# A four-layer recurrent block on one core: the down projection becomes a woven stage, and the balancing's column product is taken by rows

## What is computed

```
xn = layernorm(x)
s  = attention_L(xn)              # four different attentions
g  = silu(feed_forward_L(xn))     # four different feed-forwards
x  = x + s * g
```

```
w_eff = w * (su @ sv)
d = silu(x @ gate_eff.T) * (x @ up_eff.T)
y = d @ down_eff.T
```

## Time and profile before

| | |
|---|---|
| median of 3 runs | 1273.21 us (1271.34 to 1274.51) |
| profiled execution | 1270.83 us, span 1268.8 us |
| granted TensorE clock, mean of the span | 0.908 |
| PE busy | 1050.2 us, 83% |
| DVE busy | 834.3 us, 66% |
| ACT busy | 565.0 us, 45% |
| POOL busy | 328.4 us, 26% |

### The profile page before, as it was taken

How to read it: one execution, slowest core, us unless ns; L and a number is a source line. 1 busy time by engine, 2 the same in 40 slices (tenths; PEclk the granted TensorE clock), 3 DMA queues, 4 the chain that set the end, 5 groups by cost and what they waited for, 6 DMA issues and landing times.

```text
span 1268.8 us, 19873 instructions
## 1 busy us (share of the span) xinstructions
PE 1050.2 (83%) x7480; PEld 444.8 (35%) x7480; DVE 834.3 (66%) x1475; ACT 565.0 (45%) x797; POOL 328.4 (26%) x516
## 2 busy tenths in 40 slices
PE   2889999897898997865535639899899988999998
PEld 2434444343333444531211302223233234434344
DVE  6322222001786884798997999888978787876874
ACT  2533333100565664502123335858645767354671
POOL 2145444001776311000002136360000042011230
PEclk9989999998698998786657758999999999999999
DMA  8421220001321011020000032140012111220200
GB/s 306 143 73 55 72 75 25 1 1 49 89 64 35 26 37 60 14 63 22 16 0 1 27 102 74 48 148 28 20 35 69 51 44 39 64 76 26 69 17 34
DMA packets 54899, 69.72 MB, mean 55 GB/s; under 512 B 9526, under 2 KB 43444, under 8 KB 54800
## 3 DMA queue, kind: packets, MB, share of 16 engines
q1 hardware_dynamic: 50828, 58.57, 14.7%
q0 software_dynamic: 3984, 9.98, 2.8%
HBM read 49.45 MB, written 18.82 MB: 54 GB/s over the span
## 4 chain that ended last, share of the span: by engine, by line
DVE 30%; PE 30%; issue 4%; ACT 4%; POOL 3%; DMA 3%; SPq 1%; ACTq 0%; DVEq 0%; POOLq 0%
DVE w_mx L1320 14%; PE w_banks L667 8%; PE w_po L1250 7%; PE w_banks L1230 4%; PE w_banks L1202 3%; DVE w_region L1933 2%; ACT w_pr L1270 2%; PE w_banks L1190 2%; PE w_banks L1584 2%; DVE w_region L1893 1%; DVE w_region L1930 1%; DVE w_region L1928 1%; DVE w_region L1926 1%; DMA w_ks<-stack_scratch 1%; DVE w_region L1924 1%
## 5 line engine op out<-in xcount | busy, mean ns | idle before, releaser
L1320 DVE TENSOR_REDUCE w_mx<-w_banks 128x2 f32<-128x1024 f32 (+3 forms) x352 | 368.6, 1086 | 94.0 <-PE w_banks L1202 92.6
L1270 ACT ACTIVATE w_pr<-w_banks 128x1024 f32<-128x1024 f32 (+1 forms) x312 | 304.2, 1014 | 214.3 <-PE w_banks L1230 201.9
L1308 POOL TENSOR_SCALAR_AFFINE_SELECT w_pr<-w_pr 128x512 f32<-128x512 f32 (+1 forms) x184 | 107.8, 591 | 396.1 <-ACT w_pr L1270 396.1
L1230 PE MATMUL w_banks<-w_qs,w_ks 49*128 49x512 f16 (+7 forms) x832 | 125.4, 346 | 42.9 <-DVE w_mx L1320 30.3
L1202 PE MATMUL w_banks<-w_ks,w_qs 48*128 48x512 f16 (+7 forms) x832 | 139.4, 351 | 25.1 <-DVE w_mx L1320 11.3
L1250 PE MATMUL w_po<-w_pr,w_vz 128*17 128x512 f32 (+7 forms) x1152 | 142.8, 533 | 17.1 <-DVE w_vz L909 6.7
L78 PE MATMUL f_pp<-xt,sl_region 128*128 128x512 f16 x672 | 149.2, 383 | 2.4 <-POOL sl_region L504 2.4
L480 DVE TENSOR_TENSOR sl_region<-sl_region,f_pp 128x512 f32<-128x512 f32 x28 | 19.3, 688 | 120.3 <-ACT sl_region L495 120.3
L78 PEld LDWEIGHTS f_pp<-xt,sl_region 128*128 128x128 f16 x672 | 65.2, 99 | 83.8 <-issue 5.6
L1230 PEld LDWEIGHTS w_banks<-w_qs,w_ks 49*128 49x128 f16 (+1 forms) x832 | 36.0, 97 | 147.1 <-issue 58.3
L1190 PE MATMUL w_banks<-mask_half,ident_half 64*128 64x128 bf16 (+1 forms) x768 | 64.7, 248 | 17.9 <-DMA w_ks<-stack_scratch 8.6
(11 more groups left out here) (221 smaller groups left out, 1478.9 us busy)
## 6 DMA issues: line engine op xcount, KB each, us to landing
stack_scratch<-sl_region SPq DMA_DIRECT2D x102, 128.0 KB
w_qs<-stack_scratch SPq DMA_DIRECT2D x96, 96.0 KB, 2.3
sl_region<-in_L_gu SPq DMA_DIRECT2D x14, 512.0 KB
w_stage<-in_L_w POOLq DMA_DIRECT2D x36, 128.0 KB, 2.4
sl_region<-in_L_down SPq DMA_DIRECT2D x14, 256.0 KB
stack_scratch<-p_qk SPq DMA_DIRECT2D x24, 128.0 KB
w_ks<-stack_scratch SPq DMA_DIRECT2D x32, 96.0 KB, 2.5
bw_stage<-in_L_w SPq DMA_DIRECT2D x4, 640.0 KB, 10.1
```

The source lines that it names most:

```text
L1230: mm = pe.matmul(g.banks.pair_at(f)[:, half, at:at + T - q0], g.ks[base:base + self.rows + 1, k_slot, k_place, j * P:(j + 1) * P], g.qs[ba ...
L1270: act.activation(g.probs.at(self.pr_fill[s])[:, :, 0:width], g.banks.pair_at(self.s_fill[s])[:, :, 0:width], ACT.Exp, scale=self.a.scale). ...
L1308: pool.affine_select(out=diagonal, in_=diagonal, compare_op=ALU.is_ge, fill=0.0, base=0, pattern=pattern, channel_multiplier=-1).then_inc( ...
L1320: dve.tensor_reduce(out, g.banks.pair_at(self.m_fill[m])[:, :, 0:heads * keys].rearrange("q h (p k) -> q h p k", k=keys), AX.X, ALU.max).t ...
```

## The change

1. `swiglu_low_rank` no longer has the phase d0. It calls `finish(dt, wd)`, which runs a new block, `down_and_maxima`.
2. In that block the down projection is a stage `Down` of 89 ticks, 11 for each of the 8 tiles (four matmuls each, two in the last) and one for the last silu. It is merged, by a table of its own, with the first 4 ticks of q, 18 of m and 3 of t of the first attention: three groups' maxima. The block has parts for PE, ACT, DVE and SP.
3. `clear_semaphores` still follows `first_layer`, and `weave` begins behind it. The weave's strands leave out the ticks already done (`rest_of`). Queries, keys, maxima and the PSUM banks of the weave are allocated before the first layer; otherwise the body of `weave` is the same, with its indentation changed.
4. Balancing's column product writes its tile row by row, with the inverses broadcast over the rows.
5. The table `TURNS` is new. The old one begins with ten w ticks, the new one with 2, then l, then 27. By count of ticks, balancing's first step stands in the old table where the projection p11 (layer 1, second batch) begins, and its last step 11 ticks of s ahead of the outward product o10 (layer 1, first batch), with that layer's scores and values all done. In the new one 41 steps stand ahead of p11, and o10 starts 6 steps before balancing's end, with 12 e and 16 v ticks of layer 1 still to come.

```diff
-        sl = view(g.sl_region, 0, (NT, D), F32)
-        with Phase(nc, "d0", "made silued") as (block, made, silued), \
-                nc.psum_tensor("d0_pf", [P, 4, BANK], F32) as pf:
...
-                for t in range(NT):
-                    wait_pos(pe, silued, t - 3)
-                    product(pe, pf[:, t % 4, :], lambda part, j: dt[:, part, j, t * P:(t + 1) * P],
-                            lambda part, j: wd[:, part, j, :], range(n_i)).then_inc(made, 1)
...
+        finish(dt, wd)
...
+class Down(Stage):
...
+        self.parts = -(-self.chunks * len(PRODUCTS) // 4)
+        s = g.signals
+        self.made, self.out = s.take("d_made", NT), s.take("d_out", NT)
+        self.ticks = range(NT * self.parts + 1)
...
+        mm = partial(pe, self.g.banks.at(self.fills[i]), lambda part, c: self.gated[:, part, c, i * P:(i + 1) * P],
+                     lambda part, c: self.w[:, part, c, :], range(self.chunks), PRODUCTS, 4 * k, 4 * k + 4)
+        if k == self.parts - 1:
+            mm.then_inc(self.made.sem, 1)
+
+    def act(self, act, t):
+        i, k = divmod(t, self.parts)
+        if k == 0 and i > 0:
+            act.wait_ge(self.made.sem, self.made.at + i)
+            act.activation(self.sl[:, i - 1, :], self.g.banks.at(self.fills[i - 1]), ACT.Silu).then_inc(self.out.sem, 1)
...
         elif step == 5:
-            op = dve.tensor_tensor(bycol, bycol, inverse.rearrange("p (t j) -> p t j", j=n).unsqueeze(3)
+            whole = both.rearrange("p t (i j) -> p t i j", j=n)
+            op = dve.tensor_tensor(whole, whole, inverse.rearrange("p (t j) -> p t j", j=n).unsqueeze(2)
                                    .to_broadcast([P, NT, n, n]), ALU.mult)
...
+FIRST_TURNS = "q4 d6 " + "m1 d5 " * 6 + "t1 " + "m1 d5 " * 6 + "t1 d2 " + "m1 d3 " * 6 + "t1 d3"
+
 TURNS = """
-    w10 m5 q m2 q2 l m t m q m3 e m e t m e m e m2 v e m v e q e v t w2 q e o m2 v m e m v m e2 o m w v e2 w v m w e
...
+    w2 l w27 e q e2 q e2 v e2 v2 m e m2 e2 v m2 o m v o e2 v m e v e v m o m t m v e o v2 e m v o m q e2 o m2 t e m
...
+def rest_of(stage, emitted):
+    return stage, [t for t in stage.ticks if (stage, t) not in emitted]
...
         load_constants(nc, g, ins)
-        first_layer(nc, g, ins, x_tiles, by_chunk)
+        first_layer(nc, g, ins, x_tiles, by_chunk, lambda gated, w: down_and_maxima(nc, top, g, stacks[0], gated, w))
         clear_semaphores(nc)
         weave(nc, top, g, ins, out, stacks, by_chunk, sign_region, sign_qkv, sign_o)
+
+
+def down_and_maxima(nc, top, g, stack_dram, gated, w):
+
+    banks = top.enter_context(nc.psum_tensor("w_banks", [P, 7, BANK], F32))
+    g.po = top.enter_context(nc.psum_tensor("w_po", [P, BANK], F32))
...
+    down = Down(g, gated, w, view(g.sl_region, 0, (NT, D), F32))
+    g.first = first = Attend(g, g.heads[0], 0, g.vz0[:, 0:NI, :, :], g.att[:, 0:NI, :], stack_dram, None, None)
+    order = []
+    merge({"d": [all_of(down)], "q": [some_of(first.stacks, 0, SLOTS + 1)], "m": [some_of(first.maxima, 0, SLOTS * first.n_m)],
+           "t": [some_of(first.turns, 0, SLOTS)]}, FIRST_TURNS, order, g.emitted, g.banks)
+    with nc.Block() as block:
+        @block.tensor
...
+        @block.scalar
...
+        @block.vector
...
+        @block.sync
...
```

More of the change, by code:

```diff
@@ L1941 @@
[L1941 to L1950, removed]
@@ new lines, in split_rows, with done @@
+    def split_rows(name, dst, chunks=KC):
+        return [(by_chunk(name, chunks)[:, c, :], dst[:, 0, c, :], dst[:, 1, c, :]) for c in range(chunks)]
+    def done(stage):
+        return stage.normed, stage.groups
+    a00 = g.first
+    a01 = Attend(g, h[0], 1, vz(0, 1), att(1), stacks[0], None, a00)
+    split1 = Split(g, split_rows("L0_wo", wo) + split_rows("L1_w", w1)
+                   + split_rows("L1_wo", wo1, 2) + split_rows("L1_w24", w24) + [(ins["L1_wb"], wb[:, 0], wb[:, 1])])
+    o00 = Outward(g, h[0], 0, lambda part, c: wo[:, part, c, :], o_rows[:, 0, :], att(0), sl[:, 0], done(a00), None,
+                  [split1.done(), small.done()])
@@ new lines, in weave @@
+    n20 = Normalise(g, 0, (o10.added, NI), att(0))
+    p20 = Project(g, h[2], 0, lambda part, c, cols: sign_qkv[:, c, cols], g.binary.cols, g.binary.rows[:, 0:h[2].n_v],
+                  vz(2, 0), n20, stacks[2], [])
+    a20 = Attend(g, h[2], 0, vz(2, 0), att(0), stacks[2], p20, a11)
+    split2 = Split(g, split_rows("L2_w_ra", w_ra) + [(ins["L2_w_b"], w_b[:, 0, :], w_b[:, 1, :])])
+    o11 = Outward(g, h[1], 1, lambda part, c: wo1[:, part, c, :], o_rows[:, 1, :], att(1), sl[:, 1], done(a11),
+                  s1.ready(), [])
@@ new lines, in weave @@
+    n21 = Normalise(g, 1, (o11.added, NI), att(1))
+    p21 = Project(g, h[2], 1, lambda part, c, cols: sign_qkv[:, c, cols], g.binary.cols, g.binary.rows[:, 0:h[2].n_v],
+                  vz(2, 1), n21, stacks[2], [])
+    a21 = Attend(g, h[2], 1, vz(2, 1), att(1), stacks[2], p21, a20)
+    r20 = Routed(g, 0, w_ra, w_b, 1, sl[:, 0], n20, [split2.done(), small.done()], [(o10.gated, NI)])
+    split3 = Split(g, split_rows("L3_w", w3) + split_rows("L3_wo", wo),
+                   [(p11.made, len(p11.chunks)), (p11.v_made, p11.v_units), s1.ready(), (o01.made, NI)])
@@ new lines, in weave @@
+    p30 = Project(g, h[3], 0, lambda part, c, cols: w3[:, part, c, cols], col3, v_row3[:, :], vz(3, 0), n30, stacks[3],
+                  [split3.done(), rows3.done(), small.done()] + rope_free, rope=True)
+    a30 = Attend(g, h[3], 0, vz(3, 0), att(0), stacks[3], p30, a21)
+    r21 = Routed(g, 1, w_ra, w_b, 1, sl[:, 0], n21, [], [(o20.gated, NI)])
+    r21.begins_after = [(o20, o20.ticks[-1])]
+    split_base = Split(g, split_rows("L3_w_base", w_base), [(o11.gated, NI)])
+    o21 = Outward(g, h[2], 1, lambda part, c: sign_o[:, c, :], g.binary.rows[:, h[2].n_v:], att(1), sl[:, 0], done(a21),
+                  r21.ready(), [])
@@ L2291, in lay_out @@
+    nc.clear_and_free_semaphores(list(g.signals.sems.values()))
+    nc.all_engine_barrier()
 def lay_out(v):
```

301 lines of the change are left out of this document (147 added, 154 removed).

## The result

The changed kernel takes **1292.82 us** (median of 4 runs, 1288.56 to 1294.16) against 1272.28 us of the kernel before on the same chip (4 runs, 1271.23 to 1274.51): a ratio of 1.0153, with a 95% interval of 1.0124 to 1.0183. It is slower by 20.5 us. The profiled execution took 1291.59 us with a span of 1289.9, 21.1 us above the span of before.

The account below looks back on a forecast made before the run. The limit was taken to change by stage: PE in the down projection and until 462 us, DVE in balancing. 1270.8 + 7.5 + 33.8 - 5 - 4.5 - 3.5 = 1299.1, plus 2.4 for the median: 1301.5 us, range 1279 to 1320.

Parts of the forecast that it names:

- a stretch after the first v that is over 20 us shorter than the 936 us it has now: Stretch behind the first value product: shortening by over 20 us was listed among signs that would prove the prediction wrong.
- Part 1: Down projection woven with 18 maxima: reductions free, PE pays for units and transposes, +7.5 us.
- Part 2: Start of the weave: all 29 pieces ahead of the first mask delay the first value product, +33.8 us.
- rival (a): POOL finishes its pieces under the down projection, first value product at 320.7; median 1248 us, chance 0.05.
- what part 1 saves is swallowed whole by this wait: Start of the weave: startup and maxima saved would have been nearly 20 us, but the wait behind the pieces takes it.
- The recovery after the wait costs again what it costs now: PE's clock behind the first value product: recovering after the wait was to cost the same as before.
- Part 3: From 333 to 462 us: nineteen pieces fewer among the masks, PE's waits and part of a clock dip go, -5 us.
- Part 4: Balancing's column product written row by row: 50 products on DVE's chain, each 0.090 us shorter, -4.5 us.
- Part 5: Rest of the new table: order around balancing closes some two fifths of DVE's 9.0 us mixing gap, -3.5 us.
- rival (b): New table repays the wait: below the old time, chance 0.04; partial repayment of 10 to 20 us more, about 1286, 0.11.
- central forecast: Whole kernel: 1291 to 1311 us, with a chance of 0.60.
- Rival (c): The wait is there, nothing given back behind it: 1310 us, up to 1320, chance 0.20.

Follow-up runs that it names:

- Experiment 12: Kernel with 17 pieces split under the down projection, its down stage now alternating two maxima with twenty down matmuls, halving stream changes: 1239.76 us, one run.
- experiment 1: Kernel before, with all 29 weight pieces moved to the head of its old table and nothing else changed: 1303.24 us, ratio 1.0247.
- experiment 10: Changed kernel with 17 weight pieces split by POOL under the down projection and the other 12 spread in the weave: 1241.32 us, ratio 0.9743.
- experiment 4: Changed kernel with the old table, less the ticks already done, so ten pieces stand ahead of the first mask: 1277.88 us, ratio 1.0038.
- experiment 7: Kernel before with only balancing's column product written row by row: 1268.05 us, ratio 0.9974.
- experiment 5: Changed kernel with the old table, less the ticks already done, and the 29 pieces spread behind every fourth m, e and v tick: 1261.75 us, ratio 0.9905.
- 2: Changed kernel with its new table, only the 29 pieces spread one behind every fourth tick of m, e and v: 1248.33 us, ratio 0.9806.
- experiment 6: Kernel before with two transposition ticks of maxima moved 10 and 6 ticks earlier in its old table: 1266.39 us, ratio 0.9958.
- 9: Kernel before with its own ten pieces and the other 19 spread one behind every fourth tick: 1268.56 us, ratio 0.9978.

## Why the prediction was right, and which terms were off

The direction, the mechanism of the loss and the range held: 1301.5 forecast, 1292.8 measured, in 1279 to 1320. One of the prediction's own signs of being wrong came true all the same: "a stretch after the first v that is over 20 us shorter than the 936 us it has now". It was 910.5, shorter by 25.3. So the account of the head was right, and the account of what follows it, 13 us, gave only half of what the run showed. Point by point:

- **Part 1, +7.5, was 10.0.** The reductions were free, as argued: no wait of PE on DVE in the stage, although all 18 stand in it. The stacks' load was covered by the six ticks. What failed is the step "a unit's mask and score matmuls advance by ...": from start to next start the units in the stage take 0.44 and 0.55 us (the two small ones), 0.39 and 0.44 (the wide ones), 7.95 in all, and behind each the down matmuls lose 0.1 us again. In the earlier trace rows a unit stands beside others of short matmuls; a price read there does not hold the change to and from a stream of 128x512 ones. Experiment 12 bears this out in one run: half the changes, and 1.9 us of the stage are gone.
- **Part 2, +33.8, was 35.2**, and 34.6 in experiment 1. The pace of 2.01 us held (325.26 to 327.25; the 24th copy began at 371.53, 23 steps of 2.01). The first load landed 2.0 us later after its issue (5.31 us from issue to copy, 3.30 in the earlier trace rows), a term that the sum lacked. Against it, the 5.7 for the narrow pieces counted from a DMA issue that the pace from copy to copy already holds (0.56 us): from the copy at 373.54 to the mask at 378.61 they took 5.07. That POOL would not start early held too: the rival (a) needs the part for POOL that experiment 10 adds. The sentence "what part 1 saves is swallowed whole by this wait" is what experiment 4 shows.
- **"The recovery after the wait costs again what it costs now"** was wrong to the good side: 3.6 us of work at the lower level, as the last section shows.
- **Part 3, -5, was -3.4**, and the pieces are not what gave most of it. The waits on masks did go, as forecast: behind the first value product the changed kernel has none. But between that product and the normalisation it is 94.27 us before and already 91.85 in experiment 4, which still has pieces among the masks. That 2.4 goes with a granted clock of 0.98 for 0.94; the last 1.0 is what is left for the missing pieces and the new order together.
- **Part 4, -4.5**, was right: 291 ns for 382, 50 times. The strided order is slower by a third at fp32. The Trainium skill ("VectorE: DVE Perf Modes", Mode 1x) would have both orders at the same rate; experiment 7 and both profiles speak against that here.
- **Part 5, -3.5, was some -17**, by far the largest miss: 18.0 by the profiles of experiment 4 and the changed kernel, 13.4 by the medians of 5 and 2. The step that failed is "counted out, the old and new tables ... differ around balancing". I compared tables from balancing on and read no waits from 427 to 520. There the kernel before had its own 5.21 us wait for placed maxima, and lost clock behind it (0.96, and 1.00 without the wait); a view of the waits over that stretch names it in its first line. Another 6.7 us came inside balancing (experiment 5 against 2, both with the new column product): 3.4 of it is less DVE work between the first and the last step (112.65 us busy for 109.23), the rest less idle time of DVE. And 4.4 us came behind layer 2's first normalisation (5.0 from 5 to 2), where the prediction had the tables "nearly side by side". The gap of 9 us among the mixing products, from which the term was taken, is not where the gain lies: from the end of balancing to layer 2's normalisation the changed kernel took 1.1 us more, though DVE stood idle 4.2 us there for 8.0 before. But for the one wait of experiment 6, what gains in the new order is read from windows and not isolated by a run.
- **The partial repayment in rival (b)**, 10 to 20 us more than 13, is what happened by its size: 25.3 instead of 13, so 12.3 more. The head cost 46.4 instead of 41.3, 5.1 more, and the median of the runs lay 1.2 above the profiled execution instead of 2.4: 1301.5 - 12.3 + 5.1 - 1.2 = 1293.1, against the 1292.8 measured. Part of the closeness is luck, two misses of opposite sign: had the head cost what was forecast, the time would have been some 1288, below the 1291 to 1311 of the central forecast. Rival (c) is refuted by experiments 4 and 5.

The sum again with measured terms, against the profiled execution: 1268.8 + 1.0 + 10.2 + 35.2 - 25.3 = 1289.9.

## What to carry to other kernels

In an order that every engine follows strictly, work of low urgency costs by where it stands, not by how long it is: the same 29 pieces made PE wait 56 us ahead of the first mask and some 5 when spread among the masks, and 17 of them cost nothing to be seen under a stage in which their engine was idle. Moving work off an engine's path pays only if nothing else ends at the same place, so look, before moving, for the second chain that ends there (here POOL's ten pieces beside PE's maxima), and shorten both. When a whole table is new, read the waits of the old order over every stretch, not just where the counts differ: one late transposition cost 5 us there, and moving two letters got it back.

## What the runs showed of the hardware that was not expected

**After one long stop PE was back at full clock sooner than among short stops.** The windows of the kernel before and of the changed one after PE's first value product:

```profile
322.00:326.00 4.00, 2.60 (x18) 0.89 (x20) 3.92 (x4) 1.27 (x2) 3.23 (x7) 0.50 0.43 126
326.00:330.00 4.00, 3.64 (x35) 1.80 (x31) 2.47 (x3) 2.20 (x3) 3.23 (x7) 0.50 0.25 67
...
336.00:339.00 3.00, 3.00 (x29) 0.77 (x29) 1.23 (x1) 2.28 (x3) 1.05 (x2) 0.68 0.21 66
339.00:342.00 3.00, 2.61 (x46) 1.30 (x46) 2.47 (x3) 2.75 (x5) 2.36 (x5) 1.00 0.19 51
```

```profile
381.00:383.00 2.00, 2.00 (x20) 0.63 (x20) 0.00 (x0) 1.06 (x2) 0.16 (x1) 0.50 0.00 0
383.00:385.00 2.00, 1.80 (x30) 0.84 (x24) 0.80 (x2) 1.53 (x2) 0.82 (x2) 1.00 0.04 8
```

Before, PE worked with short stops and was granted half speed (1.2 GHz) from 314 to about 337, 23 us of which it was busy 18.62. In the changed kernel it stood idle for 56 us, then worked without a stop from 379.44 and was at full speed (2.4 GHz) from 383 on: 3.6 us of work at the lower level. The long wait cost little beyond its own length. Experiment 1 shows the same: PE idle for 36.84 us, a clock of 0.50 from 367.59 to 371 and 0.91 in the next two us. And experiment 10 shows the other side: with only short stops ahead of it, PE was busy 15.20 of the 17.90 us from 322.10 to 340, at a mean clock of 0.56.

**Changing between streams of matmuls costs PE about 0.1 us each way** (experiment 12), visible only as starts that lie further apart, not as idle time.

**The first load from DRAM after the barrier took longer behind the woven stage**: 5.31 us from POOL's issue to its first copy in the changed kernel, 5.25 in experiment 4 (319.19 to 324.44), and 3.30 in the kernel before, 3.05 in experiment 1, 3.2 in 7 and 9 and 3.0 in 6, all with the old stage and the same three loads. So it goes with the new stage and not with chance; why is open, no run was made for it.
